# Mask added by TensorE in the banks, minima of two banks at a time, exps read from banks

## The reference

```python
# x (64, 32, 512), ctx (64, 257, 512), mask (64, 1, 1, 257): 1.0 where a key is masked, else 0.0
qh = split_heads(layernorm(x) @ Wq + bq)        # 16 heads of 32
kh = split_heads(ctx @ Wk + bk)
vh = split_heads(ctx @ Wv + bv)
logits = einsum('bhqd,bhkd->bhqk', qh, kh) / sqrt(32)
attn = softmax(logits + mask * -1e9)
x = x + (attn @ vh) @ Wo + bo
x = x + mamba(layernorm(x))     # 1024 channels, 16 states, a scan over 32 positions
x = x + ffn(layernorm(x))       # 512 -> 2048 -> 512, quantised
```

## Time and profile before

| | us |
|---|---|
| median of 3 runs | 2039.79 (2039.04 to 2040.78) |
| profiled execution | 2034.94 |
| its span | 2033.2 |
| TensorE busy (matmuls) | 1902.7, 94% |
| VectorE busy | 1851.3, 91% |
| ScalarE busy | 1682.3, 83% |
| GpSimd busy | 494.9, 24% |
| score passes on VectorE (L1697) | 93.2 and 21.0 for their accumulator reads, 256 of them |
| exps on ScalarE (L1296) | 127.3 and 50.9 for their accumulator reads, 256 of them |
| mask scaling on GpSimd (L1517) | 137.8, 64 of them |

### The profile page before, as it was taken

The page is one execution under the profiler, slowest core; times in us unless marked ns, Lnnn a source line. Parts: engine busy times, 40 slices in busy tenths (PEclk is TensorE's granted clock), DMA queues, the critical chain, the costliest instruction groups (busy, mean ns, idle before and its releaser), DMA issues. The chain is left out here.

```text
span 2033.2 us, 37605 instructions
## 1 busy us (share of the span) xinstructions
PE 1902.7 (94%) x11661; PEld 1350.1 (66%) x11676; DVE 1851.3 (91%) x2320; ACT 1682.3 (83%) x4617; POOL 494.9 (24%) x392
## 2 busy tenths in 40 slices
PE   7998999999999999999999999999999999668799
PEld 5576776767676666767676767666676767466444
DVE  1546999999999999999999999999999999999788
ACT  3458989898989889898989898888989898867484
POOL 1001214131414223141314142422314131201013
PEclk9999999999999999999999999999999999788899
DMA  9522333333342333333333334233333333420214
GB/s 295 213 82 89 79 93 79 92 81 96 72 114 65 83 98 73 93 83 92 77 91 82 98 72 114 62 84 93 80 93 83 91 78 88 95 84 11 73 42 145
DMA packets 93396, 188.55 MB, mean 93 GB/s; under 512 B 18768, under 2 KB 39904, under 8 KB 88160
## 3 DMA queue, kind: packets, MB, share of 16 engines
q1 hardware_dynamic: 78448, 133.32, 20.9%
q0 software_dynamic: 14832, 54.01, 14.1%
HBM read 116.12 MB, written 17.18 MB: 66 GB/s over the span
## 5 line engine op out<-in xcount | busy, mean ns | idle before, releaser
L1443 ACT ACTIVATE dA<-dt,A_sb 128x124 f32<-128x124 f32 x2048 | 617.0, 391 | 11.3 <-DVE dt L1770 10.1
L1820 DVE TENSOR_TENSOR_SCAN hb<-dA,hb 128x2048 f32<-128x2048 f32 x118 | 522.4, 4427 | 8.1 <-ACT dA L1443 4.3
L992 PE MATMUL bank<-ctxT,wk_sb 128*128 128x256 f32 x2048 | 461.6, 383 | 13.4 <-ACT ctxT L1259 11.4
L1003 PE MATMUL bank<-wv_sb,ctxT 128*128 128x512 f32 x1024 | 465.2, 595 | 2.3 <-ACT ctxT L1259 2.3
L992 PEld LDWEIGHTS bank<-ctxT,wk_sb 128*128 128x128 f32 x2048 | 382.6, 191 | 77.2 <-ACT ctxT L1259 18.2
L1003 PEld LDWEIGHTS bank<-wv_sb,ctxT 128*128 128x128 f32 x1024 | 186.6, 191 | 188.6 <-issue 185.1
L1545 POOL DMA_DIRECT2D hb<-hb x103 | 93.3, 906 | 862.5 <-DVE hb L1826 846.6
L1815 DVE TENSOR_TENSOR hb<-u,BC 128x2048 f32<-128x2048 f32 x118 | 270.4, 2292 | 5.7 <-DVE u L1782 2.6
L1826 DVE TENSOR_TENSOR hb<-hb,BC 128x2048 f32<-128x2048 f32 x117 | 268.2, 2292 | 1.5
L1096 PE MATMUL bank<-xn2T,win_sb 128*128 128x128 f32 x2048 | 236.8, 277 | 0.7 <-ACT xn2T L1358 0.7
L1096 PEld LDWEIGHTS bank<-xn2T,win_sb 128*128 128x128 f32 x2048 | 234.1, 193 | 4.5 <-issue 2.4
(11 more groups left out here) (167 smaller groups left out, 2582.2 us busy)
## 6 DMA issues: line engine op xcount, KB each, us to landing
hb<-hb POOLq DMA_DIRECT2D x103, 512.0 KB, 4.8
ctx_sb<-in_ctx_dram SPq DMA_DIRECT2D x64, 512.0 KB, 3.7
BC<-bcd_dram SPq DMA_DIRECT2D x32, 1024.0 KB, 7.0
maskb<-in_mask_Bx1x1xS_fk_dram SPq DMA_DIRECT2D x64, 128.5 KB, 3.4
wstage<-in_L_ffn_w_dram SPq DMA_DIRECT2D x4, 2048.0 KB, 11.7
x_sb<-in_x_dram SPq DMA_DIRECT2D x16, 256.0 KB, 3.5
win_sb<-in_L_attn_in_proj_w_dram SPq DMA_DIRECT2D x1, 4096.0 KB, 25.2
bo_sb<-bias_dram SPq DMA_DIRECT2D x64, 64.0 KB, 2.1
```

Of the source, the lines that this page charges most:

```text
L992: last = pe.matmul(bank[6 + j][:, (m % 2) * KF:(m % 2 + 1) * KF], wk_sb[:, c, m * P:(m + 1) * P], ctxT[:, c, :], start=(c == 0), stop=(c = ...
L1003: last = pe.matmul(bank[h][:], ctxT[:, c, h * P:(h + 1) * P], wv_sb[:, c, :], start=(c == 0), stop=(c == DC - 1))
L1443: last = act.activation(dA[:, c % 2, n * BT:(n + 1) * BT, 1:], dt[:, c, :].rearrange("p (b s) -> p b s", s=S)[:, :, 1:], ACT.Exp, scale=A_ ...
L1820: ins = dve.tensor_tensor_scan(flat, dA[:, c % 2].rearrange("p n s -> p (n s)"), flat, 0.0, ALU.mult, ALU.add)
```

## The change

The bank tensors 2 to 5 become one tensor of four banks, so that one instruction can read two of them. GpSimd sets a column of ones at the start. Before the score products of a batch TensorE waits for the scaled mask and makes four products of ones (1 row by 128 columns) with one row of the mask (257 columns), each in another group of array rows and into another bank; the score products then add to these. VectorE's four fused passes become two plain minimum reductions, each over two banks, with no result but the minima. ScalarE's exps read the banks instead of Pr and write Pr. GpSimd's mask of the next batch waits for the score products instead of the passes; mamba_turn and last_values wait for the exps instead of the passes. VectorE no longer waits for the mask or for the transposes of the batch before.

```diff
-HIGHEST = 3.0e38
...
-        bank = [ctx.enter_context(nc.psum_tensor(f"bank{i}", [P, 512], F32)) for i in range(8)]
+        def psum(name, shape):
+            return ctx.enter_context(nc.psum_tensor(name, shape, F32))
+
+        bank = [psum("bank0", [P, 512]), psum("bank1", [P, 512])]
+        score_banks = psum("score_banks", [P, DC, 512])
+        bank += [score_banks[:, m, :] for m in range(DC)]
+        bank += [psum("bank6", [P, 512]), psum("bank7", [P, 512])]
...
                 def last_values(self):
-                    pe.wait_ge(scored, DC)
+                    pe.wait_ge(exp_done, DC)
...
                     if isinstance(g, int) and g == 0:
                         pe.wait_ge(kcol_ready, 1)
+                        pe.wait_ge(setup_pool, 3)
...
+                    pe.wait_ge(mask_scaled, g + 1)
                     apart(pe)
+                    for m in range(DC):
+                        row = slice(m * DEPTH, m * DEPTH + 1)
+                        pe.matmul(bank[2 + m][:, 0:KEYS], consts[row, 1:2].broadcast_to([1, P]), maskn[row, :],
+                                  start=True, stop=False)
                     for j in range(HC):
                         for m in range(DC):
                             rows = slice(m * DEPTH, (m + 1) * DEPTH)
                             last = pe.matmul(bank[2 + m][j * S:(j + 1) * S, 0:KEYS], Q[rows, j, b * S:(b + 1) * S],
-                                             KT[rows, j, 0:KEYS], start=True, stop=True)
+                                             KT[rows, j, 0:KEYS], start=False, stop=True)
...
                     pe.wait_ge(ln_done[1], t + 1)
-                    wait(pe, scored, keys - DC)
+                    wait(pe, exp_done, keys - DC)
...
-            act.wait_ge(setup_pool, 2)
+            act.wait_ge(setup_pool, 3)
...
                 def softmax(self, g):
                     for m in range(DC):
-                        act.wait_ge(scored, DC * g + m + 1)
-                        act.activation(Pr[:, m, :], Pr[:, m, :], ACT.Exp, scale=-1.0, bias=soft[:, 0, m:m + 1],
+                        act.wait_ge(scored, 2 * g + m // 2 + 1)
+                        act.activation(Pr[:, m, :], bank[2 + m][:, 0:KEYS], ACT.Exp, scale=-1.0, bias=soft[:, 0, m:m + 1],
                                        accum_out=soft[:, 1, m:m + 1]).then_inc(exp_done, 1)
...
             pool.memset(dA[:], 0.0).then_inc(setup_pool, 1)
+            pool.memset(consts[:, 1:2], 1.0).then_inc(setup_pool, 1)
...
-                    wait(pool, scored, DC * g)
+                    wait(pool, qk_psum, DC * g)
                     pool.wait_ge(mask_loaded, 16 * (g + 1))
...
-                def score_pass(self, g, m):
-                    dve.wait_ge(qk_psum, DC * g + m + 1)
-                    apart(dve)
-                    dve.tensor_tensor_reduce(Pr[:, m, :], bank[2 + m][:, 0:KEYS], maskn[:], 1.0, HIGHEST,
-                                             ALU.add, ALU.min, soft[:, 0, m:m + 1]).then_inc(scored, 1)
-
                 def scores(self, g, t, b, to):
 
-                    wait(dve, pt_psum, 2 * g)
-                    dve.wait_ge(mask_scaled, g + 1)
-                    apart(dve)
-                    for m in range(DC):
-                        self.score_pass(g, m)
+                    for m in (0, 2):
+                        dve.wait_ge(qk_psum, DC * g + m + 2)
+                        dve.tensor_reduce(soft[:, 0, m:m + 2], score_banks[:, m:m + 2, 0:KEYS], AX.X, ALU.min
+                                          ).then_inc(scored, 1)
```

## The result

| | before | after |
|---|---|---|
| median, us | 2039.41 (4 runs, 2037.44 to 2040.78) | 2057.05 (4 runs, 2053.78 to 2058.43) |
| ratio of after to before | | 1.0085, 95% interval 1.0067 to 1.0102 |
| profiled execution, its span | 2034.94, 2033.2 | 2056.16, 2054.4 |

The changed kernel is slower by 17.6 us in the medians (predicted 19.6) and by 21.2 us between the two profiled executions. In the code of after the mask products are L1031, the score products L1036, the reductions L1710, the exps L1307, the reciprocal L1715, the mask scaling L1529, mamba_turn L1100, the scan's product, scan and product with C L1820, L1825 and L1831.

A forecast was written before the change was run, and what follows sets the result against it. A ring through TensorE, VectorE, ScalarE, SyncE and GpSimd bounds the kernel. Mask products paid in b=1 and b=2 make 16.6 us over 14 tiles, plus 3.0 in the first two: +19.6, 2059.4 us, range 2042 to 2080.

The forecast's parts named there:

- The ring: TensorE from mamba_turn to b=2 scores, VectorE to b=3 scores, ScalarE to xn3T, SyncE, GpSimd, TensorE again: sets the tile period.
- x: Time the four mask products add on TensorE in each batch: 0.65 us, taken from the score block.
- the bounds 0.23 and 0.44: Lower sizes for a batch's mask products: 0.23 us if blocks share well, 0.44 us without a drain at the mode change.
- VectorE's reductions, exps, waits: Per tile, without the mask products: first exp +0.27, exps from banks -0.14, paired reductions -0.16, together -0.03 us.
- The mask on GpSimd, the releases: TensorE's wait for the scaled mask, tightest in b=3 with 12.5 us of cover, and the new bank releases: no cost.
- Sum: 1.24 us in each of 14 tiles, less 0.8, plus 3.0 in the first two tiles: +19.6 us.
- The wait in b=2: Sign of being right: VectorE's reduction in b=2 waits about 1.2 us for TensorE's score products.
- A: Rival: on TensorE the mask products run one after another, 1.75 us a batch, 2104 us; chance 0.12.
- B: Rival: no difference, mask products slip under the score block's own 0.21 us, about 0.1 a batch, 2042 us; chance 0.08.
- C: Rival: faster, VectorE alone sets the pace and all four of its gains count, -9, 2031 us; chance 0.06.

The follow-up runs named there:

- e1: Changed kernel with the mask products in b=0 and b=3 alone, the mask left out of b=1 and b=2: 2034.80 us, ratio 0.9985.
- e2: Changed kernel with the mask products in b=1 and b=2 alone, the mask left out of b=0 and b=3: 2057.73 us, ratio 1.0102.
- e9: Changed kernel with the mask products made twice in b=0 and b=3, once in b=1 and b=2: 2058.93 us, ratio 1.0094.
- e5: Changed kernel with mask and ones as bf16 in the mask products: 2045.15 us, ratio 1.0025.
- e3: Changed kernel with no mask products at all, the mask left out: 2035.66 us, ratio 0.9992.
- e10: Changed kernel with a semaphore increment put between VectorE's wait and each reduction: 2058.67 us, ratio 1.0092.
- e6: Changed kernel with the next tile's bias rows loaded in b=1 instead of behind xn3T's store: 2041.33 us, ratio 1.0013.
- e7: Kernel before the change with the next tile's bias rows loaded in b=1 instead of behind xn3T's store: 2035.13 us, ratio 0.9984.
- e8: Changed kernel with both bf16 mask products and the earlier load of the bias rows: 2028.39 us, ratio 0.9955.
- e4: Kernel before the change with the mask products added and nothing else, so the mask is added twice: 2056.76 us, ratio 1.0093.
- e12: e7 plus VectorE's layernorm statistics ahead of the b=0 score passes and its reciprocal behind the scan's product: 2040.72 us, ratio 1.0004.

## Why the prediction was right, step by step

**The ring.** Right. TensorE gapless from mamba_turn to b=2, VectorE waiting for the banks in b=2, and the cost in b=1 and b=2 alone (e1, e2). That b=0 and b=3 hide their products is shown by e1, to within the 0.08 us between after and e2; e9 shows where the cover ends: with a block of 1.08 us instead of 0.64, 0.28 us a tile come through.

**The size of x.** Predicted 0.65 from the score block, measured 0.64 to 0.65 wherever the clock is full. The reading behind it, two rounds of 0.22 us and about 0.21 for the change of shape, is what e9 shows (0.44 and 0.20). With that the bounds 0.23 and 0.44 fall, and the Trainium skill's rule that a change of tiling mode drains TensorE ("TensorEngine Tiling (Array Packing)", Tiling Modes) agrees with the row. The 0.20 us are no constant, though: in bf16 the whole block takes 0.22 (e5). The estimate by the Trainium skill's speedup of four row groups ("TensorE: Matmul & The Clock Gate", Part 3) gave 0.57, somewhat short.

**VectorE's reductions, exps, waits.** Right in sign and too small: predicted -0.03 us a tile without x, measured some -0.2 (e3 from tile 3 on, and e1). The terms: two reductions hold VectorE 1.21 us (predicted 1.23, from 1.39); the exps start 0.72 us behind the first reduction in b=3 (predicted 0.69); an exp keeps ScalarE busy for 463 ns (118.6/256) where it took 497 (127.3/256 in the table of before), 0.034 us less against the 0.04 that were read from a neighbour. Not foreseen was the increment that vanished with the fused pass, 0.11 us in VectorE's favour at each visible wait (e10, whose period is 0.06 us longer than that of after). Where the rest of the difference comes from was not traced.

**The mask on GpSimd, the releases.** Costed at nothing, and nothing is seen: no wait of TensorE on GpSimd in the groups. Once scaled in 4.27 us, the mask for b=3 of tile 9 now takes 0.42 (from 1083.19), and nobody waited for either. The long one had begun while VectorE's scan ran (from 1069.59) and ended with it; the short one ends before the scan at 1084.05 begins.

**Sum.** Between tile 2 and tile 15 predicted 13 x 1.24 - 0.8 = 15.3 us, measured 15.4. A tile was to cost 1.24 us, less the 0.8 spread over 13, so 1.18, and costs 1.18. That it meets to a hundredth is in part luck: the first of the 13 intervals grows by 2.10 us (109.70 to 111.80), the other 12 by 1.11 in the mean, about what 2 x 0.64 less the 0.2 of the paragraph on VectorE gives. Up to b=2 of tile 2 predicted 3.0 + 1.24 = 4.2, measured 5.5. The windows show a part of it that no prediction of the kernel could give (columns as in the earlier trace rows); the kernel before, then after:

```profile
60.00:80.00 20.00, 20.00 (x147) 13.68 (x147) 12.71 (x24) 10.47 (x30) 2.22 (x4) 0.94 0.56 192
```

```profile
60.00:80.00 20.00, 20.00 (x114) 14.04 (x111) 12.53 (x18) 9.11 (x27) 2.23 (x4) 0.84 0.54 191
```

The granted clock is 0.84 instead of 0.94 in 20 us in which TensorE never idles: some 2 us, as an estimate. It is a mixture of the two levels. From 60 to 61 us 0.50 is granted, the lower one (1.2 GHz), and the mask block of tile 0, b=1, which lies there, takes 1.17 us (59.68 to 60.85) instead of 0.64. That clock differs between executions of kernels whose work is the same up to there, 0.84 in after and 1.00 in e6, 0.94 in before and 0.88 in e7, and on one chip 0.91 in e5 and 1.00 in e8, so it is no property of the change. In e6 and e10 the lower level came earlier (0.89 from 30 to 45 us). In e10, with 1.00 from 60 to 80 us, b=2 of tile 2 comes at 300.54, 3.5 us later than in before (which had 0.94), on the other side of the predicted 4.2. That the profiled executions differ by 21.2 us and the medians by 17.6 is of the same kind: the profile of before had been 4.85 us under the median that the prediction used, that of after is 0.89 under its own.

**The wait in b=2.** Predicted about 1.2 us, measured 0.64: the mark that missed, while the period of 111.35 is just under its 111.4 to 111.5. The rest is in b=1, where VectorE now waits 0.72 us for ScalarE's xpad, which TensorE delays in turn: ScalarE's copy of the keys ahead of it waits 1.03 us for L997, and did not wait at that place before. Both waits are the same 1.3 us that TensorE runs late, met in two places; a reader who had judged the theory by the b=2 wait alone would have called it half wrong.

**Rivals.** A (one after another, x = 1.75) falls with the block of 0.64 us. B (no difference, x about 0.1) falls with the same row and with e4. C (faster, VectorE alone setting the pace) needed mamba_turn to come earlier by more than 2x; it comes later against the x1 write, 8.56 us (1354.96 to 1363.52) in tile 12, where it was 8.35 (1338.89 to 1347.24). It came back in another form: once x was 0.22 and the GpSimd chain shortened (e8), the changed kernel is the faster one.

## What to carry to other kernels

When two engines' ways around a loop are equally long, work moved from the one to the other is paid in full by the receiver and gives the donor only idle time: find which stretch of the receiving queue has no gap, and count how many of the moved pieces land in it, not how many there are. Before moving an operation ahead on one engine, read what it is put ahead of: in e12 3 us won on GpSimd were lost to an operation of ScalarE that stood earlier in its queue. A cheap data type for a constant term (e5, 0.92 us a tile) and a load issued earlier (e6, 1.05) were worth more here than the exchange of the operations itself.

## What the runs showed of the hardware

- Four products of one row by 128 columns in four row groups, 257 columns of fp32: 0.64 us between products of other shapes, 0.44 us for four more behind them (e9). In bf16 the four hold TensorE 0.22 us (e5). At a granted clock of 0.52 the fp32 block took 1.17 us (after, tile 0).
- A semaphore increment between VectorE's wait and its instruction delays the start by 0.11 us, 1.01 against 0.90 us behind the scores' start (e10).
- GpSimd operations on 128 numbers, 0.2 to 0.6 us by themselves, last 2.25 to 2.4 us when they meet VectorE's product of 2048 elements (the rows of after and e6).
- An exp of 128 x 257 with its sum keeps ScalarE busy for 463 ns when it reads a bank and for 497 ns when it reads SBUF (after, before).
- TensorE's granted clock was 0.84 to 1.00 in the same 20 us of tile 0, by the execution and not by the change, which moves a profile by some 2 us. Between tiles 2 and 15 an interval with a mean of 0.97 to 0.99 is 0.6 to 5.5 us longer than its neighbours (e1, e2, e3, e4, e5, e12), enough to hide an effect of 0.2 us a tile.
